# Input statistics of a four-block kernel on DVE's moments operation, with the weight preparation placed in other stages

## What is computed

```
def _gn(v, G=32, eps=1e-05):
    g = v.reshape(B_, H_, W_, G, C_ // G)
    m = jnp.mean(g, axis=(1, 2, 4), keepdims=True)
    s = jnp.var(g, axis=(1, 2, 4), keepdims=True)
    return ((g - m) / jnp.sqrt(s + eps)).reshape(v.shape)
# blocks 0, 1, 3 (triangle blocks); xn = layer_norm(x) * w + b
left, right = [(xn @ W + b) * sigmoid(xn @ Wg + bg) for each side]
out   = einsum('bkjd,bkid->bijd', left, right)
out   = (layer_norm(out) * w2 + b2) @ Wo + bo
return out * sigmoid(xn @ Wgo + bgo)
# block 2: layer norm, then two linear layers whose inputs and weights
# are rounded to fp8 with a scale per row, with relu(a) * b between them
for each of the four: x = x + block(_gn(x))
```

## Time and profile before

| what | value |
|---|---|
| median of 3 runs | 1777.76 us (1776.29 to 1778.16) |
| the profiled execution, device time | 1780.16 us |
| its span in the trace | 1778.4 us, 30667 instructions |
| PE busy | 1331.0 us (75%) |
| DVE busy | 1383.3 us (78%) |
| ACT busy | 1167.7 us (66%) |
| POOL busy | 1001.5 us (56%) |
| granted TensorE clock, mean | 0.907 |
| first group norm's last wait ends (`gn_ready`) | about 98.6 us from the start |

### The profile page before, as it was taken

The page is one execution under the profiler, slowest core; times in us unless marked ns, Lnnn a source line. Parts: engine busy times, 40 slices in busy tenths (PEclk is TensorE's granted clock), DMA queues, the critical chain, the costliest instruction groups (busy, mean ns, idle before and its releaser), DMA issues.

```text
span 1778.4 us, 30667 instructions
## 1 busy us (share of the span) xinstructions
PE 1331.0 (75%) x9712; PEld 797.9 (45%) x9712; DVE 1383.3 (78%) x3708; ACT 1167.7 (66%) x2680; POOL 1001.5 (56%) x701
## 2 busy tenths in 40 slices
PE   5558888798688879798899657666675577778765
PEld 1123337665433349565677323333333233337654
DVE  6978871598688851898599899999999577761598
ACT  2358881598588851898343377777776288871598
POOL 7379960387699920687455214444445687740354
PEclk8879999899899999899899858989999799998789
DMA  7025436377545553677244124444445334435477
GB/s 263 0 78 119 120 88 155 99 222 208 142 107 119 120 120 77 182 227 208 89 110 113 33 54 110 105 108 107 106 109 119 96 100 107 100 78 133 135 256 249
DMA packets 408833, 225.53 MB, mean 127 GB/s; under 512 B 343456, under 2 KB 343776, under 8 KB 408672
## 3 DMA queue, kind: packets, MB, share of 16 engines
q1 hardware_dynamic: 270240, 185.81, 38.7%
q10 hardware_dynamic: 138432, 37.76, 9.1%
HBM read 114.97 MB, written 66.06 MB: 102 GB/s over the span
## 4 chain that ended last, share of the span: by engine, by line
issue 28%; DVE 21%; POOL 21%; ACT 16%; PE 12%; DMA 1%; SPq 0%; POOLq 0%; ACTq 0%; DVEq 0%
ACT work L1012 12%; POOL ln_s L514 6%; DVE stats L725 5%; PE ps L1131 5%; POOL work L506 4%; POOL work L520 4%; PE ps L1248 4%; POOL work L474 3%; POOL sg_all L549 2%; PE ps L1160 2%; DVE pairs L783 2%; ACT work L1025 2%; DVE stats L809 1%; DVE work L641 1%; ACT work L994 1%
## 5 line engine op out<-in xcount | busy, mean ns | idle before, releaser
L514 POOL TENSOR_TENSOR ln_s<-ln_s,half_power 128x8 f32<-128x8 f32 x216 | 356.4, 1650 | 355.7 <-DVE ln_s L734 305.2
L1173 PE MATMUL ps<-wfold,work 64*128 64x320 f32 x1728 | 342.6, 488 | 98.8 <-DVE pairs L783 52.8
L1131 PE MATMUL ps<-work,ones 128*128 128x512 f32 x504 | 280.6, 673 | 59.8 <-ACT work L970 49.5
L1012 ACT ACTIVATE work<-pairs,ln_s 128x64 f32<-128x64 f32 x648 | 263.4, 497 | 19.1 <-DVE ln_s L741 19.1
L1012 ACT ACTIVATE work<-work,ln_s 128x64 f32<-128x64 f32 x576 | 212.4, 430 | 95.4 <-DVE ln_s L741 95.2
L1173 PEld LDWEIGHTS ps<-wfold,work 64*128 64x128 f32 x1728 | 139.0, 190 | 270.6 <-DVE pairs L783 133.1
L783 DVE TENSOR_TENSOR pairs<-ps,work 128x256 f32<-128x256 f32 x288 | 169.0, 597 | 63.3 <-ACT work L1025 58.3
L1025 ACT ACTIVATE work<-ps 128x384 f32<-128x384 f32 x432 | 194.4, 476 | 4.9 <-PE ps L1173 3.8
L1160 PE MATMUL ps<-ident,work 128*128 128x128 f32 x864 | 147.7, 298 | 47.2 <-DVE work L752 28.8
L994 ACT ACTIVATE work<-ps 128x512 f32<-128x512 f32 x216 | 129.2, 598 | 72.1 <-PE ps L1160 70.5
L1072 ACT ACTIVATE pairs<-pairs,rescale 128x256 f32<-128x256 f32 x288 | 122.5, 498 | 71.3 <-DVE work L914 71.3
(11 more groups left out here) (148 smaller groups left out, 2636.0 us busy)
## 6 DMA issues: line engine op xcount, KB each, us to landing
work<-x_mid SPq DMA_DIRECT2D x144, 256.0 KB, 2.9
gate_dram<-work ACTq DMA_DIRECT2D x108, 256.0 KB, 2.8
work<-gate_dram SPq DMA_DIRECT2D x108, 256.0 KB, 3.2
work<-in_x_in SPq DMA_DIRECT2D x72, 256.0 KB, 2.9
work<-x_nat SPq DMA_DIRECT2D x144, 128.0 KB, 3.0
x_mid<-work SPq DMA_DIRECT2D x72, 256.0 KB, 2.6
work<-pairs SPq DMA_DIRECT2D x96, 96.0 KB, 3.0
work<-pairs ACTq DMA_DIRECT2D x96, 96.0 KB, 3.2
```

The costliest lines, as they stand in the source:

```text
L514: pool.tensor_tensor(ln_s[:, b, RSTD, :], ln_s[:, b, VAR, :], half_power[:, 0:U], ALU.pow)\
L1012: last = act.activation(dst[:, r % dst.shape[1], u * C:(u + 1) * C], src, ACT.Identity, scale=ln_s[:, b, RSTD, u:u + 1], bias=ln_s[:, b, S ...
L1131: last = pe.matmul(ps[:, bank, :], ones[:], src[:, b, :], start=first, stop=end, skip_group_check=True)
L1173: last = pe.matmul(ps[:, PAIR_BANKS[n % 3] + odd, 0:PROJ], xnT[rows, b, pair * P:(pair + 1) * P], wfold[rows, q, 0:PROJ], start=True, stop ...
```

## The change

Before block 0, the anchor, the shift, the squares, the accumulator and the PE sums of squares are gone. DVE runs its moments operation (`bn_stats`, shown as BATCH_NORM_STATS2 or BN_STATS) on each of the 32 groups of each of four loads of nine tiles, 128 instructions over 144 values per partition (72 positions x 2 channels). Each gives two counts, means and sums of squared distances, for even and odd values. `sums_of_input` adds the means, has PE sum them over the partitions, takes the distance of each partial mean from the mean, and has a second PE sum make the variance. The `anchor` that later blocks use is now the mean of the groups.

The input is loaded in four transfers of 2304 KB, the first ahead of the parameters. The weights of block 0 are scaled between the second and third load's moments, and their biases are folded in behind the first group norm. The weights of blocks 1 and 3 are scaled by DVE between the channel products of block 0, summed by PE behind the last product, and their biases are folded at the end of block 0's output stage. The weights of block 2 are loaded at the start of block 1's output stage (SP, behind a POOL memset), rounded at its end (DVE and one ACT instruction), transposed by PE behind it, and split into parts by DVE in block 2, behind its group norm. Some small arrays lie in the large buffer instead of tiles of their own.

```diff
-WHOLE = [(0, 1), (1, 6), (6, 12), (12, 18), (18, 24), (24, 30), (30, 36)]
-SUM_PARTS = [(0, 4), (4, 8), (8, 12), (12, 16), (16, 36)]
+IN_COUNT = 72.0
+WHOLE = [(9 * k, 9 * k + 9) for k in range(4)]
...
-            sp.dma_start(x_all[:, 0, :], x_in[0]).then_inc(x_whole[0], 16)
+            def load_whole(k):
+                lo, hi = WHOLE[k]
+                sp.dma_start(x_all[:, lo:hi, :], x_in[lo:hi].rearrange("t p f -> p t f")).then_inc(x_whole[k], 16)
+            load_whole(0)
             sp.dma_start(wfold[:], weights).then_inc(s_params, 16)
...
-            sp.wait_ge(s_const, 1)
-            sp.dma_start(wq_raw[:, 0:512], w1).then_inc(s_params, 16)
-            sp.dma_start(wq_raw[0:C, 512:768], w2).then_inc(s_params, 16)
-            for k, (lo, hi) in enumerate(WHOLE[1:]):
-                sp.dma_start(x_all[:, lo:hi, :], x_in[lo:hi].rearrange("t p f -> p t f")).then_inc(x_whole[k + 1], 16)
+            for k in range(1, len(WHOLE)):
+                load_whole(k)
...
+                    if l == 1:
+                        sp.wait_ge(wq_cleared, 1)
+                        sp.dma_start(wq_raw[:, 0:512], w1).then_inc(wq_loaded, 16)
+                        sp.dma_start(wq_raw[0:C, 512:768], w2).then_inc(wq_loaded, 16)
...
-            pool.wait_ge(anchor_ready, 1)
-            for k, (lo, hi) in enumerate(WHOLE):
-                pool.wait_ge(x_whole[k], 16)
-                pipeline(pool, [(0, shift_input)], hi - lo, lo)
...
+                if l == 0 and t == 0:
+                    pool.wait_ge(s_fold_pe, 3)
+                    pool.wait_ge(anchor_ready, 1)
...
+                    if l == 1:
+                        pool.wait_ge(chan_done, CHANNEL_PAIRS * BLOCKS * (q + 1))
+                        pool.memset(wq_raw[:, 512:768], 0.0).then_inc(wq_cleared, 1)
...
-            dve.wait_ge(anchor_sum, 1)
-            dve.tensor_reduce(gn_s[:, 7, :], ps[:, 0, :].rearrange("p (u g e) -> p g u e", u=U, e=2), AX.XY, ALU.add)\
-                .then_inc(anchor_step, 1)
-            dve.wait_ge(anchor_step, 1)
...
+            def quantise_weights():
+                w1_rows = lambda ap: ap[:, 0:512].rearrange("p (k c) -> p k c", k=4)
+                dve.wait_ge(wq_loaded, 32)
...
+                chain(dve.tensor_scalar(wq_y[:, 512:768], wq_raw[:, 512:768], wscale[:, 2, 4:5], None, ALU.mult), 5)
+                dve.wait_ge(s_quant_abs, 1)
+                chain(dve.tensor_scalar(wq_magic, wq_magic, SUBNORMAL, None, ALU.max), 6)
...
+                chain(dve.tensor_scalar(wq_y[:, 512:768], wq_q[:, 512:768], wscale[:, 1, 4:5], None, ALU.mult), 9)
+            def split_weights():
+                dve.wait_ge(s_quant_pe, 1)
...
+                    chain(dve.tensor_copy(dst[:, 0, :], ps[:, bank, 0:width]), n - 4)
+                    chain(dve.tensor_tensor(rest, ps[:, bank, 0:width], dst[:, 0, :], ALU.subtract), n - 3)
+                    chain(dve.tensor_copy(dst[:, 1, :], rest), n - 2)
+                    chain(dve.tensor_tensor(rest, rest, dst[:, 1, :], ALU.subtract), n - 1)
+                    chain(dve.tensor_copy(dst[:, 2, :], rest), n)
+            def scale_weights(q, tmp):
+                dve.tensor_scalar(tmp[:, 0:PROJ], wfold[:, q, 0:PROJ], nrm_d[:, q, 0:1], None, ALU.mult)
+                dve.tensor_scalar(tmp[:, PROJ:], wfold[:, q, PROJ:], nrm_d[:, q, 1:2], None, ALU.mult).then_inc(s_fold, 1)
                 dve.tensor_scalar(wfold[:, q, 0:PROJ], wfold[:, q, 0:PROJ], nrm[:, q, 0:1], ROOT_C, ALU.mult, ALU.mult)
                 dve.tensor_scalar(wfold[:, q, PROJ:], wfold[:, q, PROJ:], nrm[:, q, 2:3], ROOT_C, ALU.mult, ALU.mult).then_inc(s_fold, 1)
+            def fold_biases(q, bank, tmp, steps):
                 dve.wait_ge(s_fold_pe, q + 1)
-                dve.tensor_tensor(fold_tmp, ps[:, 1, 0:PROJ + C], wbias[:, q, :], ALU.add).then_inc(s_fold, 1)
-                dve.wait_ge(s_fold, step + 3)
-                dve.scalar_tensor_tensor(out=wfold[:, q, :], in0=fold_tmp, scalar=ROOT_C / C, in1=wfold[:, q, :],
+                dve.tensor_tensor(tmp, ps[:, bank, 0:PROJ + C], wbias[:, q, :], ALU.add).then_inc(s_fold, 1)
+                dve.wait_ge(s_fold, steps)
+                dve.scalar_tensor_tensor(out=wfold[:, q, :], in0=tmp, scalar=ROOT_C / C, in1=wfold[:, q, :],
...
-            def accumulate(t, b):
-                dve.wait_ge(shift_ready, t + 1)
-                    dve.wait_ge(input_acc, t - 1)
-                    dve.tensor_tensor(acc, acc, whole_tile(t), ALU.add).then_inc(input_acc, 1)
-            pipeline(dve, [(0, accumulate)], TILES - 1, 1)
+            def moments_of_input(k):
+                lo, hi = WHOLE[k]
+                dve.wait_ge(x_whole[k], 16)
+                flat = x_all[:, lo:hi, :].rearrange("p t (u g e) -> p (t u) g e", u=U, e=2)
+                for g in range(GROUPS):
+                    last = dve.bn_stats(in_stats[:, k, g, :], flat[:, :, g, :])
+                last.then_inc(in_moments, 1)
+            def sums_of_input():
+                parts = in_stats[:].rearrange("p k g (e s) -> p g k e s", s=3)
+                each = lambda what: parts[:, :, :, :, what]
+                four = lambda ap: ap.rearrange("p g (k e) -> p g k e", k=4)
+                dve.wait_ge(in_moments, 4)
+                dve.tensor_reduce(in_sums[:, 0, :], each(1), AX.XY, ALU.add).then_inc(in_step, 1)
+                dve.wait_ge(in_summed, 1)
+                dve.tensor_scalar(gn_s[:, 2, :], ps[:, 0, 0:GROUPS], 1.0 / (P * 8), None, ALU.mult).then_inc(in_step, 1)
+                dve.wait_ge(in_step, 2)
+                for k in range(4):
+                    last = dve.tensor_tensor(four(in_far)[:, :, k, :], parts[:, :, k, :, 1],
+                                             gn_s[:, 2, :].unsqueeze(2).to_broadcast([P, GROUPS, 2]), ALU.subtract)
+                last.then_inc(in_step, 1)
+                dve.wait_ge(in_step, 3)
+                dve.tensor_tensor(in_far2[:], in_far[:], in_far[:], ALU.mult).then_inc(in_step, 1)
+                dve.wait_ge(in_step, 4)
+                for k in range(4):
+                    last = dve.scalar_tensor_tensor(out=four(in_far)[:, :, k, :], in0=four(in_far2)[:, :, k, :], scalar=IN_COUNT,
+                                                    in1=parts[:, :, k, :, 2], op0=ALU.mult, op1=ALU.add)
+                last.then_inc(in_step, 1)
+                dve.wait_ge(in_step, 5)
+                dve.tensor_reduce(in_sums[:, 1, :], in_far[:], AX.X, ALU.add).then_inc(in_step, 1)
+            moments_of_input(0)
+            moments_of_input(1)
+            dve.wait_ge(s_params, 16 * 5)
+            dve.tensor_scalar(mlp_wb[:, 0, :], mlp_wb[:, 0, :], ROOT_C, None, ALU.mult)
+            dve.tensor_tensor(nrm_d[:], nrm[:, :, 1:4:2], nrm[:, :, 0:3:2], ALU.subtract).then_inc(s_fold, 1)
+            dve.wait_ge(s_fold, 1)
+            scale_weights(0, fold_tmp[:, 0, :])
+            moments_of_input(2)
+            moments_of_input(3)
+            sums_of_input()
...
-                dve.wait_ge(sums_ready, sum_base(l))
                 if l == 0:
-                    dve.wait_ge(input_summed, 1)
...
+                    dve.wait_ge(in_summed, 2)
+                    dve.tensor_scalar(gn_s[:, 5, :], ps[:, 1, 0:GROUPS], 1.0 / GN_COUNT, GN_EPS, ALU.mult, ALU.add).then_inc(gn_step, 5)
+                    dve.wait_ge(gn_step, 5)
+                else:
+                    dve.wait_ge(sums_ready, sum_base(l))
...
+                mean = gn_s[:, 2, :].unsqueeze(2).to_broadcast([P, GROUPS, 2])
+                if l == 0:
+                    dve.tensor_copy(anchor[:].rearrange("p (g e) -> p g e", e=2), mean).then_inc(anchor_ready, 1)
+                    step(dve.tensor_copy(gn_mean[:].rearrange("p (g e) -> p g e", e=2), mean), 6)
+                else:
+                    step(dve.tensor_tensor(gn_mean[:].rearrange("p (g e) -> p g e", e=2), anchor[:].rearrange("p (g e) -> p g e", e=2),
+                                           mean, ALU.add), 6)
...
+                dve.wait_ge(s_fold, 13 if q else 5)
                 if q == 0:
-                    dve.wait_ge(s_fold, 13)
...
+                if l == 0:
+                    fold_biases(0, 2, fold_tmp[:, 0, :], 4)
...
+                        if l == 0 and k in (2, 4):
+                            scale_weights(k // 2, fold_ein[:, k // 2 - 1, :])
...
+                    if l == 0:
+                        for k in range(2):
+                            fold_biases(k + 1, 2 + k, fold_tmp[:, k, :], 10 + 2 * k)
+                    if l == 1:
+                        quantise_weights()
                 else:
+                    split_weights()
...
-            def square_input(t, b):
-                act.wait_ge(shift_ready, t + 1)
-                wait_free(act, sums_ready, t - 1)
-                apart()
-                act.activation(squares[:, b, :], whole_tile(t), ACT.Square).then_inc(sq_ready, 1)
...
+                    if l == 1:
+                        act.wait_ge(s_quant, 5)
```

(28 more changed lines are left out.)

153 lines of the change are left out of this document (59 added, 94 removed).

## The result

The changed kernel takes 1735.5 us in the median of 4 runs (1732.08 to 1738.9); the kernel before took 1777.96 us in runs beside it. The ratio is 0.9767, with a 95% interval of 0.9742 to 0.9791. The profiled execution took 1738.9 us, with a span of 1737.1. Times in the views are microseconds from the start of the span.

A forecast was written before the change was run, and what follows sets the result against it. It held that DVE's chain before the first group norm, additions behind weight preparation, bounds the kernel: 1780.16 - 46.3 + 1.6 + 4.3 + 0.6 = 1740.4 us, or 1738.0 against the median, range 1732 to 1748.

The forecast's parts named there:

- pace of the moments: Before block 0: DVE's moments of 144 values, start to start, at 0.215 us, taken from the layer norm's moments.
- second load lands: Input at the start: load 1 at 21.0 us, 3 us late because transfers behind it share the stream.
- tail to the variance: Behind the last moments: reductions, two trips to PE and small DVE instructions until the variance is ready, 4.9 us.
- variance ready, gain: First group norm: variance ready at 48.0 us instead of 94.34, so 46.3 us gained.
- folding behind `gn_ready`: Block 0's bias folding behind the first group norm: one more POOL turn plus the operation, 1.6 us lost.
- blocks 1 and 3, scaling and folding: Scaling among block 0's products, folding at its output's end: 0, covered by DVE's waits; 3.3 us if folding's cover were gone.
- rounding at the boundary: Block 2 weights behind block 1's last update: 7.7 us less a 4.41 us wait, plus POOL collisions, 4.3 us lost.
- splitting: Block 2's weights in block 2: 4.4 us against a DVE wait of 3.87 us, 0.6 us lost, at most 5.7.
- The rival in which they don't overlap: Moments before block 0 take 0.296 us each, ending with the scaling at 53.4 us; total 1748 us; chance 0.10.
- the rival of strict order: Input loads land in order, load 1 at 18.0 us, 3.0 us earlier; total 1735 us; chance 0.12.
- The rivals A and D: Moments before block 0: A, no overlap, 1748 us, 0.10; D, far costlier, 1787 us at 0.6 us each, 0.03.
- The rival in which they all meet POOL: Rounding and splitting collide with POOL as at the start: 1743 us for half, 1749 for all; chance 0.14.

The follow-up runs named there:

- gap: Changed kernel with block 0's weight scaling and bias folding moved into DVE's wait for the second load; 1730.13 us, ratio 0.9733.
- quant_ein: Changed kernel with the rounding of block 2's weights moved from behind block 1's last update into block 1's product stage; 1729.54 us, ratio 0.9738.
- six_loads: Changed kernel with six loads of six tiles, 192 moments of 96 values, instead of four of nine tiles; 1739.93 us, ratio 0.9786.
- order: Changed kernel with the second input load issued ahead of the parameters; 1732.37 us, ratio 0.9745.
- prep_start: Changed kernel with rounding and splitting of block 2's weights back at the start, among the moments; 1737.48 us, ratio 0.9786.
- old_stats: Changed kernel with the former statistics back (anchor, POOL shift, ACT squares, DVE additions, PE sums), weight preparation staying moved; 1765.8 us, ratio 0.9940.
- fill: Changed kernel with 22 unused PE matmuls added behind block 3's last product; 1736.57 us, ratio 0.9770.
- all: Changed kernel with second load ahead of parameters, rounding in block 1's product stage, folding between third and fourth load's moments; 1727.04 us, ratio 0.9713.
- fill_last: `fill_more` with its unused matmuls kept in block 3 alone; 1719.06 us, ratio 0.9679.
- fill_more: `all_fill` plus 7 unused matmuls ahead of each of the first five projections in block 3's output stage; 1719.52 us, ratio 0.9649.
- again: The changed kernel once more, unaltered; 1737.91 us, ratio 0.9781.
- all_fill: `all` plus 22 unused PE matmuls behind the products of all three triangle blocks; 1725.27 us, ratio 0.9703.

## Why the prediction was right

The forecast was 1738.0 us in a range of 1732 to 1748; measured 1735.5. By the terms of the prediction:

| term | forecast | measured in the changed kernel |
|---|---|---|
| pace of the moments | 0.215 us | 0.209 |
| second load lands | 21.0 us | 20.46 |
| moments end | 43.1 us | 41.9 |
| tail to the variance | 4.9 us | 4.9 |
| variance ready, gain | 48.0, 46.3 | 46.80, 47.5 |
| folding behind `gn_ready` | 1.6 lost | 1.55 (and 1.5 back in `gap`) |
| blocks 1 and 3, scaling and folding | 0 | 0, wait 4.41 to 1.26 |
| rounding at the boundary | 4.3 lost | 4.25 (4.26 back in `quant_ein`) |
| splitting | 0.6 lost | 0.65 |

*The moments.* The pace of the layer norm's moments carried over, and so did the slope: `six_loads` shows 1.04 ns a value against the 1.1 taken. The rival in which they don't overlap needed 0.296 us each. The Trainium skill, "VectorE: DVE Perf Modes", section "The TRN2 errata — SBUF-src ops pay a fixed extra latency per instruction", by which the estimate was 306 ns, isn't borne out for a row of these: the start-to-start pace shows 59 ns above the values, not 150 cycles, which is 156 ns by the same estimate.

*The loads.* The landing at 20.46 us is near the forecast's 21.0, but its reason was wrong. The prediction took the load late because transfers behind it share the stream. What delayed it was what stood ahead. These rows of transfers have the us from issue to landing in the last column; the first two are of the kernel before, the third of the changed one:

```profile
pairs<-in_w SPq DMA_DIRECT2D x1, 64.0 KB, 7.2
pairs<-in_x_in SPq DMA_DIRECT2D x1, 1280.0 KB, 9.8
mask_sb<-in_mask SPq DMA_DIRECT2D x1, 144.0 KB, 11.0
```

Before, the 64 KB ahead of the 1280 KB load were issued at 4.0 us and landed at 11.2, and the load landed at 14.5, 3.3 us later, about its bytes' own time (3.4 us at 388 GB/s). In the changed kernel the last parameter was issued at 3.4 us and landed at 14.4, and load 1 came 6.1 us later, its own time again. So the loads land in the order of their issue, as the rival of strict order had it; only its 18.0 us was short by 2.5, since load 0 landed at 9.98 instead of 8.4 us and the parameters took 4.4 instead of 3.5 us. Why load 0 took 1.6 us more is open. That the 3 us of the forecast met this is luck. `order` agrees: without the parameters ahead of it the second load is there before DVE asks at 16.9 us. The rivals A and D let load 0 start at about 14 us, where it started at 9.98; neither came to pass, so nothing hung on it.

*The collisions.* The rounding's two collisions with POOL cost 0.96 + 0.58 = 1.5 us where one more microsecond was counted; the rest took 7.2 us where 7.7 was counted (7.2 in `prep_start` too, where it met nobody). That the two misses cancel is luck. The rival in which they all meet POOL had its argument in the rows of the start, and those belong to the load of the start: `old_stats` shows that two engines with two SBUF operands each hold one another up as long as both are at it.

*The table load.* It stood first on ACT, 1.28 us from 0.74 us on, and ACT's next work came at 59.3 us: nothing on the path, as counted.

*The sum.* With the measured terms it is -47.5 + 1.55 + 4.25 + 0.65 = -41.1 us, and from the profiled execution of before (1780.16) 1739.1; the profiled execution of after took 1738.9. But this agreement is in part luck. Ahead of block 3 the gain was 44.4 us, 3.3 more than the terms, and 47.1 in `fill`, whose code is the same up to there. The traces show where it varies. Block 0's projection stage, from its first moments to the first product, took 168.25 us before and 168.05 to 168.25 in every changed kernel. What stands behind it scatters. Block 0 as a whole, from its first moments to its last update, took 368.8 us before and 365.6 to 367.1 in the others; block 2, from group norm to group norm, took 537.7 us before, 535.8 in the changed kernel and 535.6 to 538.1 in the others. What causes the scatter is open. Behind that point 3.0 us were lost again. The output stage of block 3 spent 51 us at the 1.2 GHz level instead of 37 (last section), and at 0.2 us for each that is 2.8 of them.

*PE's clock.* The prediction said that it would be at 0.50 again at the start and would make no difference. The stretches of the changed kernel print 1.00 there, but its trace has no record of the clock before 66.3 us, and the view prints 1.00 where it has none. The matmuls tell the level. The first row is a stretch of the changed kernel, the next two are PE's in it, the last is of the kernel before at the same place, where its records say 0.50:

```profile
50.00:60.00 10.00, 0.64 (x2) 0.50 (x2) 8.03 (x18) 0.72 (x3) 7.66 (x6) 1.00 0.22 75
```

```profile
61.20 1.09 PE L1194 MATMUL ps<-ident,work 128*128 128x128 f32 x4 [10.52 <-ACT work L1045]
71.18 0.66 PE L1194 MATMUL ps<-ident,work 128*128 128x128 f32 x4
```

```profile
107.36 1.09 PE L1160 MATMUL ps<-ident,work 128*128 128x128 f32 x4 [9.05 <-ACT work L1012]
```

Four such matmuls take 1.09 us at 61 us, as before the change, and 0.66 at 71 us. So PE was at the low level there, until some 66 us, and the prediction was right in both: the projection stage took as long as before.

## What to carry to other kernels

Ahead of a point on which everything hangs, ask of each instruction of the bounding engine whether it must stand there, and where another engine's wait is long enough to take it; here each step cost nothing in a wait that was longer than it, and what stood over where the wait was shorter. The wait must still be there when other edits have moved the loads: in `all` the folding had lost it. A pace for a new instruction can be had from its nearest relative in the trace, if one takes start to start in a row of them and not the duration of one. Where runs of a kernel spread, read an edit at its own place: distances there repeated to 0.02 us (9.36, 5.10, 4.25 us in every kernel that has them), where the group norm ahead of block 3 moved by 2.7 us between kernels with the same code up to it, and the medians' runs spread by 8 us. Two profiles that agree at a point don't show that it repeats. And where a view prints a clock of 1.00, hold it against the time of matmuls of a known form.

## What the runs showed of the hardware

The low clock at the start of block 3's output stage lasts differently long in executions of the same code, and the time follows it. Over all profiles, with the time at the 1.2 GHz level worked out from stretches of 5 us behind block 3's last product, as 2 x (1 - granted clock) x 5 summed up (the last 15 us left out):

| at the low level, us | kernels | from the group norm ahead of block 3 to the end, us |
|---|---|---|
| 0 | fill_last, fill_more | 375.3, 376.4 |
| 7 | gap | 377.2 |
| 31 to 34 | again, quant_ein, prep_start, all_fill, old_stats | 380.5 to 382.5 |
| 37 | before | 383.7 |
| 48 to 51 | six_loads, changed, fill | 385.9 to 387.1 |
| 55 | all, order | 387.6, 387.7 |

That is about (387.7 - 376.4) / 55 = 0.2 us lost for each microsecond at the low level. The matmuls agree with it. At the low level a tile's take 1.06 + 2.07 us instead of 0.60 + 1.16, and PE and ACT wait for one another in turn, 0.7 us a tile each. This row is of the changed kernel:

```profile
1645.27 2.07 PE L1282 MATMUL ps<-work 128*128 128x128 f32 x8 [0.69 <-ACT work L1027]
```

The next such row starts at 1648.88, so a tile takes 3.61 us. In `fill_more` at 1.00 ACT is busy without a break, and these rows are 2.82 us apart (1655.98 and 1658.80). That makes 1 - 2.82 / 3.61 = 0.22 us lost for each microsecond at the low level.

In all profiles in which the clock fell there, a full product stage and then pauses of PE came ahead of it: 6.6 us without the filling, within which it fell, and 1.7 and 2.1 us in `fill` and `all_fill`, within the second of which it fell. With 1.7 and 0.6 us in `fill_more` and `fill_last` it stayed at 1.00. Whether it is the shorter second pause, the 35 matmuls more, or both together that keeps it, these two don't separate. What decides how long it stays down, when it has fallen, these runs don't show.
